# Moving the search for each node's last edge from the token dispatch into the first attention

## The chip, the cores and the metric

The kernel runs on one core of a Trainium2 chip. The metric is the device time of one execution in microseconds, a median over runs. The profile is one further execution with the hardware profiler on. Its engines are PE (TensorE matmul), PEld (TensorE weight load), DVE (VectorE), ACT (ScalarE), POOL (GpSimd) and SP (SyncE, which here only issues transfers).

## The reference, cut to what matters

Four images of 128 channels and 32 by 32 places (1024 places each) go through a chain of attentions, convolutions and expert layers. The parts that matter here:

```python
# first stage, for each of 4 images (n and m run over the 1024 places)
scores = einsum('bcn,bcm->bnm', q, k)
attn   = softmax(scores, axis=-1)
x      = x + einsum('bnm,bcm->bcn', attn, v)
...
# a graph attention further on: 32768 edges with 3 attributes each
eb = edge_attr @ We + be                                # one value of each of 8 heads
col_bias = jnp.zeros((H, N)).at[:, edge_index[1]].set(eb.T)
scores = scores + col_bias[None, :, None, :]
```

Where several edges point at one node, the last one in the list counts. The kernel gets the edges in reversed order, so it looks for the **first** place at which a node's number stands in the list `targets`, and then fetches that edge's three attributes. All of this depends on the inputs alone, on nothing that the stages before compute. A sparse layer between the two stages sends each of the 4096 tokens to two of 16 experts; to do so, a dispatch stage writes the tokens into slots in memory, sorted by expert.

## The kernel before, in words

The program is a chain of stages. Each is a `Stage` (lines 33 to 46): it has its own tiles and semaphores, one block with a program for each engine, and at its end all engines meet. Only then does the next stage begin; POOL clears the semaphores of the stage that ended, one instruction each, ahead of its own work in the next one.

**The first attention** is `one_head_attention` (line 264) with the name `attn0`. It goes over 4 images in a loop, and in each over 8 row tiles `t` of 128 rows. For a tile PE computes the 128 by 1024 scores (L345), DVE takes each row's maximum (L467), ACT the exponentials (L424). PE turns them, eight 128 by 128 pieces into one PSUM tile (L371), DVE copies that to SBUF (L502), PE multiplies with the values (L360), ACT scales by the inverse row sum (L400), which DVE made (`invert`, L489), PE turns the result (L352) and DVE adds it to the activations (`add_turned`, L450). The order on each engine is written out by hand. On DVE, within tile t: wait for the turned tile t, copy it, maximum of t+2, invert t, add t-2. On PE: turn t, scores t+2, multiply t, turn the output of t-1. The output of tile t-1 can be turned only when the addition of t-2 has read the PSUM bank. After the eighth tile DVE adds tiles 6 and 7. SP loads the weights and is idle from then on; POOL copies one image into `xs` at each image's start. All engines run the images as a hardware loop (`Fori`), DVE's at L453. The same function is used a second time, as `attn2`, with a causal mask and other branches.

**The dispatch** is `dispatch_tokens` (line 1577). DVE works out the slots and POOL then sends the tokens, 64 indirect transfers in a row (L1623), and waits until they have landed. ACT's queue loads the experts' weights beside it. A function handed in as `beside` adds to each engine's program what `edge_bias` (line 1462) returns:

- SP loads `raw` (128 by 256 numbers), waits until DVE packed them, stores them as 16-bit numbers, and reads them back in four chunks of 8192, each broadcast to all 128 partitions (2 MB), into two buffers `text`.
- DVE packs them (L1516 to L1525, seven instructions in a chain and two small copies), searches each chunk for eight keys a partition with `max_index` (L1529), combines the four results into one index a node (L1531 to L1539), and later masks, splits and hands over the bias (L1542 on).
- POOL fetches the attributes of the edges found, eight indirect transfers (L1509), and waits for them. They stand in POOL's order in front of the last 16 of the 64 token transfers.

The lines that matter, the wait and the search on DVE, and POOL's order:

```python
        for i in range(CHUNKS):
            dve.wait_ge(chunk_in, 16 * (i + 1))
            dve.max_index(where[:, i, :], text[i % 2][:, CHUNK:CHUNK + KEYS], text[i % 2][:]).then_inc(searched, 1)
...
            for t in range(TILES):
                if t == 3 * TILES // 4:
                    beside_gpsimd(pool)
```

Of the kernel before, what the change touches and what calls it, by code (L numbers as in the profile page):

```python
# [6 lines left out]
F32 = mybir.dt.float32  # L7
# [256 lines left out]
def one_head_attention(m, name, wq, wk, wv, bq, bk, bv, scale, causal, routed=None):  # L264
# [6 lines left out]
    with Stage(nc) as ctx:  # L271
# [16 lines left out]
        zeroed, cleared = m.sem(f"{name}_zeroed", ctx), m.sem(f"{name}_cleared", ctx)  # L288
        block = ctx.enter_context(nc.Block())
# [3 lines left out]
        def _(sp):  # L293
# [20 lines left out]

# [130 lines left out]
        def _(dve):  # L445
# [7 lines left out]
            with dve.Fori(0, B) as b:  # L453
# [36 lines left out]

                maximum(0)
# [3 lines left out]
                for t in range(T):  # L495
# [7 lines left out]
                    if t + 2 < T:  # L503
                        maximum(t + 2)
                    invert(t)
# [956 lines left out]
def edge_bias(m, name, ctx, targets, attributes, we, be, bias_parts):  # L1462
# [3 lines left out]

    nc = m.nc  # L1470
    EDGES = targets.shape[0]
    CHUNK, KEYS = 8192, N // P
    CHUNKS = EDGES // CHUNK
    sb = lambda nm, s, dt=F32: m.sb(f"{name}_{nm}", s, dt, ctx)
    raw, a, c_, short = sb("raw", [P, EDGES // P], I32), sb("a", [P, EDGES // P]), sb("c", [P, EDGES // P]), sb("short", [P, EDGES // P], U16)
    text = [sb(f"text{i}", [P, CHUNK + KEYS], U16) for i in range(2)]
    keys, where = sb("keys", [P, KEYS], I32), sb("where", [P, CHUNKS, KEYS], U32)
    place, miss, best, found, index = sb("place", [P, CHUNKS, KEYS]), sb("miss", [P, CHUNKS, KEYS]), sb("best", [P, KEYS]), sb("found", [P, KEYS]), sb("index", [P, KEYS], U32)
    rows, rowsT, wb = sb("rows", [P, KEYS, 4]), sb("rowsT", [4, N]), sb("wb", [4, HEADS])
    bias, rest, parts = sb("bias", [HEADS, N]), sb("rest", [HEADS, N]), sb("parts", [HEADS, 3, N], BF16)  # L1480
    ps, b_ps = m.psum(f"{name}_ps", [P, N], ctx), m.psum(f"{name}_b", [P, N], ctx)
    dram = nc.dram_tensor(f"{name}_targets", [EDGES], U16, kind="Internal").ap()
    loaded, packed, sent, keyed, keys_set, chunk_in, searched, indexed, ones, masked, turned, kept, summed, split, stored, dve_step = (
        m.sem(f"{name}_{x}", ctx) for x in ("loaded", "packed", "sent", "keyed", "keys_set", "chunk_in", "searched", "indexed",
                                            "ones", "masked", "turned", "kept_", "summed", "split", "stored", "dve"))
    def sync(sp):
        sp.dma_start(raw[:], targets.rearrange("(p e) -> p e", p=P)).then_inc(loaded, 16)
        sp.dma_start(wb[0:3, :], we).then_inc(loaded, 16)
        sp.dma_start(wb[3:4, :], be.rearrange("(o h) -> o h", o=1)).then_inc(loaded, 16)
        sp.wait_ge(packed, 1)  # L1490
        sp.dma_start(dram.rearrange("(p e) -> p e", p=P), short[:]).then_inc(sent, 16)
        sp.wait_ge(sent, 16)
        for i in range(CHUNKS):
            if i >= 2:
                sp.wait_ge(searched, i - 1)
            sp.dma_start(text[i % 2][:, 0:CHUNK], dram[i * CHUNK:(i + 1) * CHUNK].rearrange("(o e) -> o e", o=1).broadcast_to((P, CHUNK))).then_inc(chunk_in, 16)
# [658 lines left out]
```

## Time and profile before

| | us |
|---|---|
| median of 3 runs (2319.66 to 2326.56) | 2325.7 |
| the profiled execution | 2343.5 |
| its span, first to last instruction | 2341.3 |
| PE busy | 1735.8 (74%) |
| DVE busy | 1471.6 (63%) |
| ACT busy | 898.2 (38%) |
| POOL busy | 247.6 (11%) |
| first attention, from its first matmul to the last addition | 25.9 to 207.2 |
| dispatch, from its first load to the next stage's first load | 1219.0 to 1340.3 |

The busy shares are means over stages with quite different limits, so they don't say what a change in one stage is worth. The first attention and the dispatch are far apart in time, and each has to be read by itself: in which order its engines release each other, and which of them is the last to reach the meeting at the stage's end. A line of the timeline gives the start in us, the duration in us, the engine, the line of the program, the operation, its output and inputs, and in brackets how long the engine had been idle and what ended that.

### The profile page before, as it was taken

What the parts mean: (1) busy time and instruction counts of PE and PEld (TensorE: products, weight loads), DVE (VectorE), ACT (ScalarE), POOL (GpSimd) and SP (SyncE); (2) the same over time, 40 slices, a digit from 0 to 9 for tenths busy, and PEclk for the clock granted to TensorE, in tenths of its full rate; (3) what the DMA queues carried; (4) which work ended last, traced back from release to release, by engine and by line L of the source; (5) the groups of instructions that cost most, each with busy time, mean ns of one, the idle gap of its engine ahead of it and who ended that gap; (6) DMA issues with size and microseconds to landing.
All of it is one profiled execution on the core that took longest, in us unless ns stands there. A gap on an engine that the chain in (4) does not pass through costs nothing. (4 is left out here: it accounts for less than half of the span.)

```text
span 2341.3 us, 29974 instructions
## 1 busy us (share of the span) xinstructions
PE 1735.8 (74%) x8782; PEld 819.7 (35%) x8783; DVE 1471.6 (63%) x2899; ACT 898.2 (38%) x1709; POOL 247.6 (11%) x247
## 2 busy tenths in 40 slices
PE   5996986999999573879840199603499999995698
PEld 3774441222222122445530055301122222224576
DVE  4555896878888374366658144325587878865466
ACT  2332332666666330033310033202246666673143
POOL 0001001010001100010006500271100000100000
PEclk9997996999999765979955599856689999997699
DMA  1000244232231401030017132220802332200000
GB/s 42 1 0 11 78 162 72 39 55 47 46 67 26 71 11 45 0 140 0 0 53 246 53 85 67 63 53 30 226 9 49 66 53 51 60 13 0 19 0 36
DMA packets 116162, 125.68 MB, mean 54 GB/s; under 512 B 22675, under 2 KB 93787, under 8 KB 114155
## 3 DMA queue, kind: packets, MB, share of 16 engines
q1 hardware_dynamic: 97822, 101.91, 18.5%
q0 software_dynamic: 13088, 16.46, 2.4%
q10 hardware_dynamic: 5168, 6.29, 0.9%
q8 instruction: 41, 0.67, 0.1%
q14 instruction: 43, 0.35, 0.1%
HBM read 79.92 MB, written 44.22 MB: 53 GB/s over the span
## 5 line engine op out<-in xcount | busy, mean ns | idle before, releaser
L889 DVE TENSOR_REDUCE heads_mx<-heads_n_bank 128x1 f32<-128x1024 f32 (+2 forms) x608 | 631.6, 1081 | 176.6 <-PE heads_n_bank L777 173.4
L871 ACT ACTIVATE heads_prob<-heads_t_bank 128x512 f32<-128x512 f32 (+2 forms) x1120 | 559.1, 578 | 450.0 <-PE heads_t_bank L794 449.9
L777 PE MATMUL heads_n_bank<-heads_ks,heads_qs 96*128 96x512 bf16 (+3 forms) x1120 | 357.9, 400 | 134.0 <-DMA heads_ks<-scale_k_parts 59.5
L794 PE MATMUL heads_t_bank<-heads_qs,heads_ks 99*128 99x512 bf16 (+3 forms) x1120 | 337.0, 381 | 11.9 <-ACT heads_prob L871 8.7
L806 PE MATMUL heads_o_bank<-heads_prob,heads_vs 128*32 128x512 f32 (+2 forms) x2240 | 296.4, 603 | 5.9 <-issue 3.4
L777 PEld LDWEIGHTS heads_n_bank<-heads_ks,heads_qs 96*128 96x128 bf16 (+2 forms) x1120 | 88.3, 100 | 451.7 <-issue 170.2
L794 PEld LDWEIGHTS heads_t_bank<-heads_qs,heads_ks 99*128 99x128 bf16 (+2 forms) x1120 | 106.4, 100 | 206.3 <-ACT heads_prob L871 104.3
L345 PE MATMUL attn_s_bank<-attn_k,attn_q 128*128 128x512 f32 x256 | 123.7, 612 | 0.0
L360 PEld LDWEIGHTS attn_o_bank<-attn_v,attn_probT 128*128 128x128 f32 x800 | 97.7, 192 | 47.1 <-ACT attn_probT L406 25.4
L360 PE MATMUL attn_o_bank<-attn_v,attn_probT 128*128 128x128 f32 x800 | 102.6, 279 | 8.4 <-ACT attn_probT L406 5.0
L260 PE MATMUL ln_ps_bank<-ident,ln_xn 128*128 128x128 f32 x64 | 17.5, 429 | 121.0 <-DVE ln_xn L240 65.6
L1893 DVE SCALAR_TENSOR_TENSOR x_channels<-experts_o_bank,combine,x_channels 128x128 f32 (+1 forms) x256 | 72.5, 345 | 41.7 <-PE experts_o_bank L1849 40.3
L1789 DVE TENSOR_TENSOR experts_hid<-experts_gate,experts_hp_bank 128x256 f32<-128x256 f32 x80 | 33.7, 421 | 99.2 <-ACT experts_gate L1769 99.2
L1728 PE MATMUL experts_hp_bank<-expert_w,experts_xT 128*128 x160 | 90.7, 649 | 5.6 <-ACT experts_xT L1764 2.4
L1078 PE MATMUL in_c_bank<-padded,scale_diag 128*128 128x512 f32 (+1 forms) x198 | 85.1, 590 | 5.1 <-ACT scale_diag L1110 5.1
L205 POOL DMA_INDIRECT ln_got<-routed_y,pick_slots x64 | 61.0, 954 | 193.0 <-issue 193.0
L1849 PEld LDWEIGHTS experts_o_bank<-experts_w,experts_hid 128*128 128x128 f32 x512 | 66.8, 193 | 29.9 <-issue 23.4
L806 PEld LDWEIGHTS heads_o_bank<-heads_prob,heads_vs 128*32 128x32 f32 (+1 forms) x2240 | 45.7, 111 | 82.9 <-issue 73.1
L1868 ACT ACTIVATE experts_hid<-experts_h_bank,experts_b 128x512 f32<-128x512 f32 x64 | 44.0, 688 | 73.1 <-PE experts_h_bank L1855 73.1
L502 DVE COPY attn_probT<-attn_t_bank 128x1024 f32<-128x1024 f32 x32 | 39.2, 1225 | 49.3 <-PE attn_t_bank L371 49.3
L424 ACT ACTIVATE attn_prob<-attn_s_bank,attn_neg 128x1024 f32<-128x1024 f32 x32 | 35.7, 1115 | 89.8 <-DVE attn_neg L467 89.8
L1849 PE MATMUL experts_o_bank<-experts_w,experts_hid 128*128 128x128 f32 x512 | 69.0, 280 | 0.0
(269 smaller groups left out, 2141.7 us busy)
## 6 DMA issues: line engine op xcount, KB each, us to landing
edges_text<-edges_targets SPq DMA_DIRECT2D x4, 2048.0 KB
heads_qs<-scale_q_parts SPq DMA_DIRECT2D x60, 128.0 KB, 4.4
heads_ks<-scale_k_parts SPq DMA_DIRECT2D x60, 128.0 KB, 6.6
routed_x<-attn_zeros SPq DMA_DIRECT2D x3, 2560.0 KB, 13.3
experts_xs<-routed_x SPq DMA_DIRECT2D x24, 320.0 KB, 3.3
heads_wide<-heads_inverse_d POOLq DMA_DIRECT2D x14, 512.0 KB, 8.2
heads_qs<-edge_q_parts SPq DMA_DIRECT2D x48, 128.0 KB
heads_ks<-edge_k_parts SPq DMA_DIRECT2D x48, 128.0 KB
```

The lines of the kernel that those rows point to most:

```text
L205: pool.indirect_dma_start(out=got[:, t, i, :], out_offset=None, in_=routed.y, in_offset=bass.IndirectOffsetOnAxis(ap=slots[:, t:t + 1], ax ...
L345: last = pe.matmul(s_ps[t % 2][:, h * 512:(h + 1) * 512], q[:, t * P:(t + 1) * P], k[:, h * 512:(h + 1) * 512], start=True, stop=True)
L360: last = pe.matmul(o_ps[:, 0:C], probT[t % 2][:, j, :], v[:, j, :], start=(j == 0), stop=(j == n - 1))
L777: last = pe.matmul(ps[0:TN, i * CH:(i + 1) * CH], query(b, slice(0, KB), s, h, j, t * TN, TN), key(b, slice(0, KB), s, j, i * CH, CH), sta ...
L794: pe.matmul(t_ps[i][0:TN, 0:CH], key(of, slice(0, KM), c // NH, j, t * TN, TN), query(of, slice(0, KM), c // NH, c % NH, j, 0, CH), start= ...
L806: last = pe.matmul(o_ps[SLOT * j:SLOT * (j + 1), 0:CH], vs[:, of if whole else 0, t, (4 * s + j) * SLOT:(4 * s + j + 1) * SLOT], prob[i][: ...
L871: act.activation(to[:], t_ps[score_bank(of, place, j)[0]][0:TN, 0:CH], ACT.Exp, scale=scale).then_inc(exped, 1)
L889: dve.tensor_reduce(mx[:, u % UC:u % UC + 1], bank()[0:TN, 0:n], AX.X, ALU.max, negate=True).then_inc(first_used, 1)
L1078: last = pe.matmul(c_ps[:, c * CH:(c + 1) * CH], weights[i].diag[:, tap, :], chunk_window(r, tap, c), start=(tap == 0), stop=(tap == 8))
L1728: pe.matmul(h_ps[j % 2][:], xT[j % 2][:], w12[:, bass.ds(expert, 1), :].rearrange("p o h -> p (o h)"), start=True, stop=True).then_inc(ope ...
L1849: last = pe.matmul(o_ps[e % 2][:, t * P:(t + 1) * P], hid[e % 2][:, t * P:(t + 1) * P], w2s[:, e, :], start=True, stop=True)
L1893: last = dve.scalar_tensor_tensor(out=tile, in0=o_ps[e % 2][:, t * P:(t + 1) * P], scalar=weight, in1=tile, op0=ALU.mult, op1=ALU.add)
```

## The change

The function `edge_bias` is split. What searches goes into a class `EdgeSearch`, whose parts are put into `one_head_attention` for `attn0`; what makes the bias from the fetched attributes stays beside the dispatch.

- The chunks are of 2048 numbers instead of 8192, sixteen instead of four, one after the maximum of every second row tile (four an image). Each of the two text buffers has its own semaphore for loads.
- The packing stands on DVE in front of the first image's first maximum. The combination of the results (now sixteen) stands after the last addition of the fourth image.
- POOL makes the keys in front of the first copy of an image, and fetches the attributes after its last one; it waits for them within the first attention.
- SP's loads, the store and the chunk loads follow the weight loads of the first attention.
- DVE's loop over the images is written out (`range` in place of `Fori`), in both uses of the function.
- Eight semaphores stay with the dispatch; eleven come to the first attention.

```diff
@@ one_head_attention
+        if search:
+            search.place(ctx)
...
             sp.wait_ge(S["loaded"], 16 * (4 if causal else 6))
+            if search:
+                search.sync(sp)
...
         def _(pool):
+            if search:
+                search.prepare(pool)
...
                 pool.tensor_copy(xs[:], at(m.xnT, b + 1)).then_inc(S["staged"], 1)
+            if search:
+                search.gather(pool)
...
-            with dve.Fori(0, B) as b:
+            for b in range(B):
...
+                if search and b == 0:
+                    search.pack(dve)
                 maximum(0)
                 maximum(1)
...
                     if t + 2 < T:
                         maximum(t + 2)
+                    if search and t % 2 == 1:
+                        search.search(dve, b * T // 2 + t // 2)
                     invert(t)
...
                     for t in range(T - 2, T):
                         add_turned(b, t)
+                if search and b == B - 1:
+                    search.choose(dve)
@@ the new class
+class EdgeSearch:
+    CHUNK, KEYS = 2048, N // P
...
+    def sync(self, sp):
+        sp.dma_start(self.raw[:], self.targets.rearrange("(p e) -> p e", p=P)).then_inc(self.loaded, 16)
+        sp.wait_ge(self.packed, 1)
+        sp.dma_start(self.dram.rearrange("(p e) -> p e", p=P), self.short[:]).then_inc(self.sent, 16)
+        sp.wait_ge(self.sent, 16)
+        for i in range(self.chunks):
+            if i >= 2:
+                sp.wait_ge(self.searched, i - 1)
+            part = self.dram[i * self.CHUNK:(i + 1) * self.CHUNK].rearrange("(o e) -> o e", o=1).broadcast_to((P, self.CHUNK))
+            sp.dma_start(self.text[i % 2][:, 0:self.CHUNK], part).then_inc(self.chunk_in[i % 2], 16)
+        for i in range(2):
+            sp.wait_ge(self.chunk_in[i], 16 * self.chunks // 2)
...
+    def gather(self, pool):
+        pool.wait_ge(self.indexed, 1)
+        for r in range(self.KEYS):
+            pool.indirect_dma_start(out=self.rows[:, r, 0:3], out_offset=None, in_=self.attributes,
+                                    in_offset=bass.IndirectOffsetOnAxis(ap=self.index[:, r:r + 1], axis=0)).then_inc(self.m.gathered, 16)
+        pool.wait_ge(self.m.gathered, 16 * self.KEYS)
+        pool.wait_ge(self.ones, 1)
...
+    def search(self, dve, i):
+        if i == 0:
+            dve.wait_ge(self.keys_set, 2)
+        dve.wait_ge(self.chunk_in[i % 2], 16 * (i // 2 + 1))
+        text = self.text[i % 2]
+        dve.max_index(self.where[:, i, :], text[:, self.CHUNK:], text[:]).then_inc(self.searched, 1)
...
@@ edge_bias, dispatch_tokens: what searched is gone
-        for i in range(CHUNKS):
-            dve.wait_ge(chunk_in, 16 * (i + 1))
-            dve.max_index(where[:, i, :], text[i % 2][:, CHUNK:CHUNK + KEYS], text[i % 2][:]).then_inc(searched, 1)
...
-                if t == 3 * TILES // 4:
-                    beside_gpsimd(pool)
```

`pack` and `choose` hold the same instructions as before, on 16 results of a key instead of 4.

## Rows read from the trace of the kernel before

**Rows 1.** Stretches: length, busy time (instructions) of each engine, granted clock, DMA share, GB/s
```profile
25.00:207.00 182.00, 172.43 (x1024) 127.58 (x1024) 92.14 (x132) 60.42 (x107) 3.12 (x3) 1.00 0.00 1
1255.00:1260.00 5.00, 0.00 (x0) 0.00 (x0) 5.00 (x1) 0.00 (x0) 3.86 (x4) 0.50 0.95 361
1290.00:1295.00 5.00, 0.00 (x0) 0.00 (x0) 0.11 (x1) 0.00 (x0) 3.78 (x5) 0.50 0.16 52
```
**Rows 2.** Timeline, the end of the dispatch: POOL's transfers, the next stage's load
```profile
1299.66 1.00 POOL L1509 DMA_INDIRECT edges_rows<-attributes,edges_index  x1 [0.30 <-issue]
...
1308.52 0.95 POOL L1509 DMA_INDIRECT edges_rows<-attributes,edges_index  x1 [0.30 <-issue]
...
1310.95 1.00 POOL L1623 DMA_INDIRECT routed_x<-xn,pick_slots  x1 [1.48 <-DMA edges_rows<-attributes,edges_index]
...
1331.65 0.97 POOL L1623 DMA_INDIRECT routed_x<-xn,pick_slots  x1 [0.30 <-issue]
1340.30 6.75 SPq L1700 DMA_DIRECT2D experts_xs<-routed_x  x8
```
**Rows 3.** Timeline, one row tile of the first attention in the middle of an image
```profile
64.41 1.23 DVE L467 TENSOR_REDUCE attn_neg<-attn_s_bank 128x1 f32<-128x1024 f32 x1 [0.49 <-PE attn_s_bank L345]
65.62 0.27 DVE L450 TENSOR_TENSOR x_channels<-attn_r_bank,x_channels 128x128 f32 x1
67.36 1.23 DVE L502 COPY attn_probT<-attn_t_bank 128x1024 f32<-128x1024 f32 x1 [1.47 <-PE attn_t_bank L371]
68.64 1.99 PEld L360 LDWEIGHTS attn_o_bank<-attn_v,attn_probT 128*128 128x128 f32 x16 [0.43 <-DVE attn_probT L502]
68.88 1.95 PE L360 MATMUL attn_o_bank<-attn_v,attn_probT 128*128 128x128 f32 x16
```
**Rows 4.** Timeline, the last row tile of the first image
```profile
71.85 1.22 DVE L502 COPY attn_probT<-attn_t_bank 128x1024 f32<-128x1024 f32 x1 [3.00 <-PE attn_t_bank L371]
...
75.15 0.27 PE L352 MATMUL attn_r_bank<-ident,attn_out 128*128 128x128 f32 x1
```
**Rows 5.** Timeline, the start of the first image
```profile
25.94 6.65 PE L326 MATMUL attn_s_bank<-attn_xs,attn_w 128*128 128x512 f32 x8 [10.15 <-DMA attn_bvb<-L_conv_bv]
...
34.21 3.60 PE L345 MATMUL attn_s_bank<-attn_k,attn_q 128*128 128x512 f32 x8
34.41 1.22 DVE L459 TENSOR_TENSOR attn_v<-attn_t_bank,attn_bvb 128x1024 f32<-128x1024 f32 x1 [14.46 <-PE attn_t_bank L333]
...
36.12 1.23 DVE L467 TENSOR_REDUCE attn_neg<-attn_s_bank 128x1 f32<-128x1024 f32 x1 [0.49 <-PE attn_s_bank L345]
```
**Rows 6.** Timeline, DVE in the dispatch: packing, wait for text, searches, combination
```profile
1240.61 0.38 DVE L1516 CAST edges_a<-edges_raw 128x256 f32<-128x256 int32 x1
...
1243.45 0.23 DVE L1525 CAST edges_text<-edges_keys 128x8 uint16<-128x8 int32 x2
...
1253.59 0.09 DVE L1529 MATCH_VALUE_LOAD edges_where<-edges_text 128x8 uint16 x1 [9.91 <-DMA edges_text<-edges_targets]
...
1262.33 8.69 DVE L1529 FIND_INDEX8 edges_where<-edges_text 128x8 uint32<-128x8200 uint16 x1
...
1271.00 8.70 DVE L1529 FIND_INDEX8 edges_where<-edges_text 128x8 uint32<-128x8200 uint16 x1
...
1288.40 0.18 DVE L1531 CAST edges_place<-edges_where 128x32 f32<-128x32 uint32 x1
...
1288.83 0.40 DVE L1534 SCALAR_TENSOR_TENSOR edges_place<-edges_place,edges_miss 128x8 f32<-128x8 f32 x4
...
1289.94 0.17 DVE L1539 CAST edges_index<-edges_best 128x8 uint32<-128x8 f32 x1
```
**Rows 7.** Timeline, the end of the first attention and the next stage's first work
```profile
206.93 0.29 DVE L450 TENSOR_TENSOR x_channels<-attn_r_bank,x_channels 128x128 f32 x1 [0.59 <-PE attn_r_bank L352]
207.50 0.33 SPq L2045 DMA_DIRECT2D taps<-L_conv_dw_w  x1
...
209.00 5.44 POOL L2052 MEMSET padded<- 128x4624 f32 x3 [85.92 <-issue]
```
**Rows 8.** Timeline, DVE in the second attention, after a wait for its own result
```profile
1032.70 0.35 DVE L472 SCALAR_TENSOR_TENSOR x_channels<-attn_o_bank,attn_inv,x_channels 128x128 f32 x1 [0.16 <-DVE attn_inv L487]
```

More of the change, by code:

```diff
@@ L1480, in edge_bias @@
+def edge_bias(m, name, ctx, search, we, be, bias_parts):
+    K = EdgeSearch.KEYS
+    sb = lambda nm, s, dt=F32: m.sb(f"{name}_{nm}", s, dt, ctx)
+    rows, rowsT, wb = search.rows, sb("rowsT", [4, N]), sb("wb", [4, HEADS])
     bias, rest, parts = sb("bias", [HEADS, N]), sb("rest", [HEADS, N]), sb("parts", [HEADS, 3, N], BF16)
     ps, b_ps = m.psum(f"{name}_ps", [P, N], ctx), m.psum(f"{name}_b", [P, N], ctx)
[L1482 to L1485, printed above, removed]
+    weighted, masked, turned, kept, summed, split, stored, dve_step = (
+        m.sem(f"{name}_{x}", ctx) for x in ("weighted", "masked", "turned", "kept_", "summed", "split", "stored", "bias_dve"))
@@ L1500, in sync @@
         sp.wait_ge(stored, 16)
-    def prepare(pool):
-        pool.memset(rows[:, :, 3:4], 1.0).then_inc(ones, 1)
-        pool.iota(keys[:], pattern=[[P, KEYS]], base=0, channel_multiplier=1).then_inc(keyed, 1)
-    def gpsimd(pool):
-        pool.wait_ge(indexed, 1)
-        for r in range(KEYS):
-            pool.indirect_dma_start(out=rows[:, r, 0:3], out_offset=None, in_=attributes,
-                                    in_offset=bass.IndirectOffsetOnAxis(ap=index[:, r:r + 1], axis=0)).then_inc(m.gathered, 16)
-        pool.wait_ge(m.gathered, 16 * KEYS)
@@ L1522, in vector @@
-        dve.tensor_copy(short[:], a[:]).then_inc(packed, 1)
-        dve.wait_ge(keyed, 1)
-        for i in range(2):
-            dve.tensor_copy(text[i][:, CHUNK:CHUNK + KEYS], keys[:]).then_inc(keys_set, 1)
-        dve.wait_ge(keys_set, 2)
-        for i in range(CHUNKS):
-            dve.wait_ge(chunk_in, 16 * (i + 1))
-            dve.max_index(where[:, i, :], text[i % 2][:, CHUNK:CHUNK + KEYS], text[i % 2][:]).then_inc(searched, 1)
-        dve.wait_ge(searched, CHUNKS)
-        step(dve.tensor_copy(place[:], where[:]))
@@ L1539, in vector @@
-        dve.tensor_copy(index[:], best[:]).then_inc(indexed, 1)
-        dve.wait_ge(m.gathered, 16 * KEYS)
-        dve.wait_ge(ones, 1)
-        dve.tensor_tensor(rows[:], rows[:], found[:].rearrange("p (k o) -> p k o", o=1).broadcast_to((P, KEYS, 4)), ALU.mult).then_inc(masked, 1)
+        dve.tensor_tensor(rows[:], rows[:], search.found[:].rearrange("p (k o) -> p k o", o=1).broadcast_to((P, K, 4)), ALU.mult).then_inc(masked, 1)
         dve.wait_ge(turned, 1)
@@ L1550, in tensor @@
         pe.wait_ge(masked, 1)
-        for r in range(KEYS):
+        for r in range(K):
             last = pe.transpose(ps[0:4, r * P:(r + 1) * P], rows[:, r, :], m.ident[:])
@@ L2090, in hybrid_kernel @@
             bias_parts = nc.dram_tensor("bias_parts", [3, HEADS, N], BF16, kind="Internal").ap()
-            beside = lambda ctx: edge_bias(m, "edges", ctx, ins["targets"], ins["attributes"], ins["L3_attn_We"], ins["L3_attn_be"], bias_parts)
+            beside = lambda ctx: edge_bias(m, "edges", ctx, search, ins["L3_attn_We"], ins["L3_attn_be"], bias_parts)
             with ExitStack() as inputs:
```

95 lines of the change are left out of this document (56 added, 39 removed).

## Prediction

> **What bounds the kernel now.** The shares of busy time of the whole run don't answer this, since the two places touched lie 1000 us apart. I read the stretches first, then the timeline of each stage's end, then one row tile of the first attention, and asked each time who is last.
>
> In the dispatch the end belongs to POOL. It sends 64 token transfers, one every 1.27 us. The eight attribute fetches stand in its queue before the last sixteen of these: the first starts at 1299.66, and the token transfer behind them at 1310.95, having waited 1.48 us for their landing [rows 2]. The last token transfer is issued by 1331.65 + 0.97 = 1332.6, and the next stage's first load goes out at 1340.30 [rows 2]. DVE's search (1253.6 to 1288.3) and the index after it are ready ten microseconds before POOL comes to the fetches [rows 2, 6]. So of the whole edge work in the dispatch, only the fetches are on the path. The search of some 35 us, its packing and its 9.9 us of waiting for text are covered by POOL's own queue.
>
> In the first attention the end belongs to PE, with DVE close behind. PE is busy 172.4 of 182 us at the full clock (2.4 GHz), DVE 92.1 us [rows 1]. That leaves DVE 90 us idle, which looks like ample room. But a row tile shows how the room is cut up. DVE ends the maximum at 65.64, the inverse and the addition at 65.89, and is then idle 1.47 us until the next turned tile is there; it copies from 67.36 to 68.59, and PE's weight load, which waited for just this copy, starts at 68.64 [rows 3]. The copy is on the path of every tile, and there are 1.47 us of slack before it.
>
> **What is taken away.** Eight fetches and their wait in POOL's queue: 1310.95 - 1299.66 = 11.3 us of the path. The search, the packing and the text loads in the dispatch cost nothing there today, so their removal gives nothing, unless the token transfers get quicker. They come at the same pace, four or five begun in 5 us and 3.8 us busy, while the DMA engines are 95% busy with text and while they are 16% busy [rows 1]. So I give that nothing. Dispatch: **-11.3 us**; the bounds are -10 (the eight at 1.27 without the wait) and -12.
>
> **What is added to the first attention's tiles.** The chunk is of 2048 + 8 instead of 8200 columns. Two searches start 1271.00 - 1262.33 = 8.67 us apart [rows 6]. By columns alone one of 2056 takes 2.17 us; with some 0.1 for the fixed part I take 2.27. Sixteen are 36.3 us of DVE, against 34.7 before.
>
> For tiles 1, 3 and 5 of each image the search stands after the maximum. It starts at 65.64 in the place of rows 3 and ends at 67.91. The inverse and the addition, which used to end 0.25 after the maximum, end at 68.16, and the copy starts at 68.20 instead of 67.36, 0.84 later, and ends at 69.43. PE then multiplies from about 69.6 instead of 68.88 [rows 3], some 0.7 us late. Nothing gives this back, since PE is the next to be full. Queued behind the search are the inverse, on which ACT's scaling waits (not needed before the late multiplication), and the addition of t-2, on which the turn of the output waits (later still). 12 times 0.72 is 8.6 us. Bounds: nothing, if the search fits into idle time, and 27 us if all 2.27 count.
>
> For tile 7 there is no maximum. The copy ends at 71.85 + 1.22 = 73.07, the search at 75.34, the addition of tile 5 at 75.6, and the turn of tile 6's output, at 75.15 before, waits for it [rows 4]. That is about 0.6, four times: 2.4 us. The packing (1240.61 to 1243.68, 3.07 us [rows 6]) begins when DVE has made the values, at 34.41 + 1.22 = 35.63, and ends at 38.70; the first maximum started at 36.12 [rows 5]. The pipeline is empty then, so nothing hides it: 2.6 us.
>
> The loop written out removes register instructions on DVE. In the second attention DVE sits idle 0.16 us before each addition [rows 8]. 32 of them at 0.13 over a plain wait bound the gain at 4 us, and in the other direction the code is straight and I see no cost. Most of those lie before a wait for ACT; I take -0.5. Tiles together: 8.6 + 2.4 + 2.6 - 0.5 = **+13.1 us**.
>
> SP issues the raw load, the store and sixteen chunk loads, in a queue that held nothing after the weights; nothing is queued behind. Each chunk is asked for when the search two before is done, some 9.3 us (two tiles) before it is used. Four times as much text landed within 9.91 us of DVE's last packing instruction, store included [rows 6], so it's there in time; the DMA engines are otherwise idle [rows 1]. POOL's keys and ones come before the first image copy, while the weights are still loading (PE starts at 25.94 [rows 5]): nothing.
>
> **What is added at its end.** This is what I take as decisive. After the last addition (206.93 + 0.29 = 207.2) all engines used to meet within 0.3 us: SP loads at 207.50 [rows 7]. Now three things stand in a row there, and no engine has anything else to do:
>
> - The combination. Before, 1288.40 to 1290.11, 1.7 us [rows 6]. Four additions took 0.40; sixteen take 1.6, and three instructions are 96 columns longer (0.1 each). 1.7 + 1.2 + 0.3 = 3.2.
> - The eight fetches and their landing: 11.3, as above [rows 2].
> - POOL's way out of a stage in which it issued indirect transfers. After the last token transfer 7.7 us pass (1332.6 to 1340.30), of which the landing explains about 1.5, as after the fetches (1309.47 to 1310.95) [rows 2]. The other 6.2 us, against 0.3 in the first attention [rows 7], I put down to POOL closing its transfers, which would come again here: +5.9. Between 0 (it belongs to the dispatch alone, or to the length of its queue) and 6; nothing makes this a gain. I take 5.9, as POOL's queue holds the same kind of transfer.
> - Eleven more semaphores are cleared ahead of POOL's fill of `padded`, which starts 1.8 us after the end, behind 21 clears [rows 7]. At most 0.9; I take 0.5, since SP's twelve loads end at about the same time as the fill.
>
> End: 3.2 + 11.3 + 5.9 + 0.5 = **+20.9 us** (14 to 22).
>
> **Sum.** +13.1 + 20.9 - 11.3 = **+22.7 us** on the profiled execution's span of 2341.3, that is 2364.0. Against the median of the runs, 2325.7 (the profiled one is 0.8% longer), it is 2325.7 + 22.7 = 2348.4 us, slower by 1.0%.
>
> **A rule of the skill against this.** At the start of this stage the granted clock is at the low level (1.2 GHz): eight matmuls take 6.65 us at 25.94 and eight like them 3.60 at 34.21, after PE has worked for some microseconds [rows 5]. The packing makes PE idle 2.6 us longer just after that. If the clock fell back there, a group like the first would be paid again, 3.0 us. The Trainium skill ("TensorE: Matmul & The Clock Gate", "What's actually happening") says that the throttled state is the default and activity releases it, which speaks for such a fall in any new pause. No row of before has a pause of this length inside the stage, so I keep it as a rival.
>
> **The rivals.**
>
> *The search is free* (0.14). 90 us of DVE idle against 36.3 speaks for it; the tight copy speaks against it. 2.6 + 20.9 - 11.3 = +12.2: 2338.
>
> *The search is paid in full* (0.10). If the copy's delay grew through the wait for PE in both directions: 36.3 + 3.1 + 20.9 - 11.3 = +49: 2375. It decides where DVE has no slack before the copy; against it stand the 1.47 us in each tile.
>
> *The clock falls after the packing* (0.08). The likeliest case + 3.0: 2351.
>
> *The way out costs nothing and the search is free* (0.05). 2.6 + 15.0 - 11.3 = +6.3, within 0.3%: 2332.
>
> *Faster: the token transfers get quicker* (0.03). The one thing on the dispatch's path that could be shared with the text's 8 MB is POOL's issue of the 64 transfers. If without the text each took half its 0.97 us of writing, 64 x 0.49 = 31 us go, and the sum is -8.7: 2317. It decides from 22.7 / 64 = 0.36 us a transfer. Against it stands the equal pace beside 95% and 16% of DMA [rows 1].
>
> *The change does not do what it says*, with text late: from 9.3 us a chunk on, DVE would wait in every second tile. A chunk would need as long as four did. That lies within the "paid in full" case and gets no chance of its own.
>
> **How the numbers follow.** The likeliest case (0.60) is 2348. The range, 2334 to 2363, holds it with the bounds of the way out and of the tiles, the free search and the fallen clock; left out are the search paid in full, the quick transfers and the free way out, 0.18 together. About 0.3% (7 us) is what a measurement of this kernel can tell from no change. Faster by more than that: 0.03. Within it: 0.07 (the free way out and a little of the bounds). Slower: 0.90.
>
> **What the profile after would show.** The first maximum of the first image 2.6 us later after the values than before; in tiles 2, 4 and 6 of an image a copy that starts right behind the addition, with no idle time before it; between the last addition and the first load of the next stage some 20 us, with DVE's combination, eight fetches and then nothing for 6 us; in the dispatch 64 token transfers without a break, ending near the same 7.7 us before the next stage. I'm wrong if the copy of every second tile still shows idle time before it (free search), if the load follows the fetches at once (free way out), or if a token transfer takes clearly under 1.27 us.

## Result: slower by 1.6%, and the profile after

| | median | runs | profiled execution, its span |
|---|---|---|---|
| before | 2326.0 us (2319.66 to 2329.44) | 6 | 2343.5, 2341.3 |
| after | 2363.8 us (2354.82 to 2365.94) | 6 | 2359.3, 2357.4 |

The ratio is 1.0159 [1.0138, 1.0180], some 37 us. The forecast was 22.7 us, at 2348.4, with 2363 as the upper end of its range. On the 2325.7 us from which the forecast started the ratio gives 2362.7.

The two profiled spans differ by 16.1 us only. The stage that collects the experts' outputs, which the change does not touch, was 21 us longer in the profiled execution of before. These are its stretches in before and in after (columns: length, busy time of PE, PEld, DVE, ACT and POOL, granted clock, DMA share, GB/s):

```profile
1503.46:1617.24 113.78, 8.74 (x32) 5.72 (x32) 37.36 (x169) 8.44 (x17) 61.04 (x64) 0.50 0.15 37
```
```profile
1536.67:1629.34 92.67, 8.75 (x32) 5.72 (x32) 37.87 (x169) 8.44 (x17) 60.64 (x64) 0.50 0.18 46
```

Engine work is equal, and so are the bytes: 113.78 us at 37 GB/s and 92.67 us at 46 are 4.2 and 4.3 MB. POOL's 64 fetches in this stage took 80.2 us in before and 79.8 in after. What differs is DVE. In before it idled 3 to 10 us in front of several small instructions for which the profile names no engine of this core as the releaser, and fell behind: the stage ended 31 us after the last fetch, in after 10. What held it up stays open. In the later runs the stage took 93 us on one chip with the changed kernel and on another with the kernel before, and 112 to 114 on a third with every kernel. So it belongs to the chip or the execution, and the rest of the two profiles differs by 16.1 + 21.1 = 37.2 us.

I compare stage by stage, from the first instruction after one meeting of the engines to the first after the next:

| | before | after | difference | forecast |
|---|---|---|---|---|
| last addition of the first attention ends | 207.22 | 238.06 | +30.8 | +13.1 |
| from there to SP's first load of the next stage | 0.28 | 15.49 | +15.2 | +20.4 |
| taps stage (the fill of `padded`) | 7.77 | 8.57 | +0.8 | +0.5 |
| dispatch | 121.30 | 108.73 | -12.6 | -11.3 |

So +34.2 us lie where the change was made, and 3.0 elsewhere, of which more below.

**The tiles.** This is a row tile with a search in the second image, all rows of DVE and the TensorE rows that turn tiles (L379) and outputs (L360). Compare [rows 3]:

```profile
109.23 1.23 DVE L475 TENSOR_REDUCE attn_neg<-attn_s_bank 128x1 f32<-128x1024 f32 x1 [0.50 <-PE attn_s_bank L353]
110.37 0.08 DVE L1549 MATCH_VALUE_LOAD edges_where<-edges_text 128x8 uint16 x1
110.44 2.29 DVE L1549 FIND_INDEX8 edges_where<-edges_text 128x8 uint32<-128x2056 uint16 x1
...
112.65 0.14 DVE L497 RECIPROCAL attn_inv<-attn_rows 128x1 f32<-128x1 f32 x1
112.71 0.27 DVE L458 TENSOR_TENSOR x_channels<-attn_r_bank,x_channels 128x128 f32<-128x128 f32 x1
...
113.13 0.30 PE L360 MATMUL attn_r_bank<-ident,attn_out 128*128 128x128 f32 x1 [2.15 <-DVE x_channels L458]
...
113.35 1.06 PE L379 MATMUL attn_t_bank<-ident,attn_prob 128*128 128x128 f32 x8
...
114.45 1.23 DVE L512 COPY attn_probT<-attn_t_bank 128x1024 f32<-128x1024 f32 x1 [1.47 <-PE attn_t_bank L379]
```

DVE was to run from the search straight into the copy. Instead it is idle 1.47 us before the copy, as in before. The idle time is on TensorE, 2.15 us, and what ends it is DVE's addition at 112.71. TensorE turns output t-1 before it turns tile t+1, and for output t-1 it needs `r_ps` free, that is the addition of t-2. That addition stands behind the search. The inverse of tile t stands behind it too, but the scaling that needs it runs from 112.88 to 113.25, beside the turn at 113.13, so it isn't what the turn waited for. In before the turn that follows the addition of [rows 3], which ends at 65.89, is this one:

```profile
66.04 0.30 PE L352 MATMUL attn_r_bank<-ident,attn_out 128*128 128x128 f32 x1
```

In both kernels it starts 0.15 us after the end of the addition (112.98 and 113.13 in after). The table of waits says it for the whole stage (the us in total, how many, the longest); before, after:

```profile
PE attn_r_bank L352 <- DVE x_channels L450: 2.3, 4, 0.6
```
```profile
PE attn_r_bank L360 <- DVE x_channels L458: 21.0, 16, 2.2
```

**The clock.** In before the granted clock was 1.00 through the images [rows 1]. (That row reads 1.00 from 25.00 on although the first record of the clock in this trace is at 31.9; before it eight matmuls took 6.65 us, and eight like them 3.60 later [rows 5].) After shows falls to the lower level (1.2 GHz), of which these four stretches hold one each:

```profile
40.00:44.00 4.00, 4.00 (x12) 2.12 (x13) 1.23 (x1) 1.06 (x2) 0.00 (x0) 0.64 0.82 256
74.00:78.00 4.00, 4.00 (x13) 2.18 (x14) 1.48 (x3) 0.05 (x1) 0.00 (x0) 0.66 0.36 135
173.00:177.00 4.00, 3.15 (x11) 2.41 (x12) 1.82 (x4) 0.37 (x1) 0.00 (x0) 0.66 0.42 131
228.00:232.00 4.00, 4.00 (x21) 4.00 (x21) 0.00 (x0) 0.37 (x1) 0.00 (x0) 0.50 0.00 0
```

**The stage's end** (compare [rows 7] for where it ended, [rows 2] for the fetches), and SP's first load of the taps:

```profile
237.77 0.29 DVE L458 TENSOR_TENSOR x_channels<-attn_r_bank,x_channels 128x128 f32<-128x128 f32 x1 [0.49 <-PE attn_r_bank L360]
237.98 0.22 DVE L1554 CAST edges_spot<-edges_where 128x128 f32<-128x128 uint32 x1
...
240.67 0.17 DVE L1562 CAST edges_index<-edges_best 128x8 uint32<-128x8 f32 x1
241.15 1.19 POOL L1523 DMA_INDIRECT edges_rows<-attributes,edges_index  x1 [102.54 <-DVE edges_index L1562]
...
250.15 0.95 POOL L1523 DMA_INDIRECT edges_rows<-attributes,edges_index  x1 [0.30 <-issue]
253.55 0.33 SPq L2085 DMA_DIRECT2D taps<-L_conv_dw_w  x1
...
256.21 3.95 POOL L2092 MEMSET padded<- 128x4624 f32 x1 [5.11 <-issue]
```

Combination 2.8, fetches 10.3 to the end of the last issue (251.10), then 2.45 us to the load.

**The dispatch.** 64 token transfers from 1283.82, without a break, and the next load 7.0 us after the last (7.7 before):

```profile
1365.97 0.96 POOL L1663 DMA_INDIRECT routed_x<-xn,pick_slots  x1 [0.30 <-issue]
1373.93 2.10 SPq L1740 DMA_DIRECT2D experts_xs<-routed_x  x4
```

### The profile page after: what moved, and what is told of

It reads as the page before. It is cut to its first block and busy times, and to the rows that moved or that the text cites. A ratio compares the mean times of both kernels' runs of the same rounds, so it can differ in the third digit from the quotient of the medians.

```text
span 2357.4 us, 29740 instructions
## 1 busy us (share of the span) xinstructions
PE 1749.9 (74%) x8782; PEld 824.5 (35%) x8783; DVE 1472.9 (62%) x2935; ACT 899.9 (38%) x1709; POOL 246.7 (10%) x247
## 5 line engine op out<-in xcount | busy, mean ns | idle before, releaser
L808 PE MATMUL heads_t_bank<-heads_qs,heads_ks 99*128 99x512 bf16 (+3 forms) x1120 | 339.7, 384 | 11.3 <-ACT heads_prob L885 7.7
L353 PE MATMUL attn_s_bank<-attn_k,attn_q 128*128 128x512 f32 x256 | 123.3, 610 | 0.0
L1762 PE MATMUL experts_xp_bank<-ident,experts_xs 128*128 128x128 f32 x80 | 22.0, 279 | 83.6 <-DMA experts_xs<-routed_x 83.6
L512 DVE COPY attn_probT<-attn_t_bank 128x1024 f32<-128x1024 f32 x32 | 39.1, 1222 | 51.3 <-PE attn_t_bank L379 51.3
## 6 DMA issues: line engine op xcount, KB each, us to landing
routed_x<-attn_zeros SPq DMA_DIRECT2D x3, 2560.0 KB, 13.2
```

What stands on the lines that cost most here:

```text
L353: last = pe.matmul(s_ps[t % 2][:, h * 512:(h + 1) * 512], q[:, t * P:(t + 1) * P], k[:, h * 512:(h + 1) * 512], start=True, stop=True)
L808: pe.matmul(t_ps[i][0:TN, 0:CH], key(of, slice(0, KM), c // NH, j, t * TN, TN), query(of, slice(0, KM), c // NH, c % NH, j, 0, CH), start= ...
```

## Experiments

Each was timed beside the kernel before on one chip, but for the one with half of the transfers, of which there is one execution, its profile. The base is the changed kernel unless said otherwise. The distance from one copy (L512) to the next, tile by tile through the second image, tells most of them apart; in the changed kernel, search_after and short_search every interval with an odd number holds a search, in chunks_1024 every interval:

```
                  0     1     2     3     4     5     6   7 and next image's start
before          4.38  4.48  4.67  4.67  4.67  4.67  4.49  11.65
changed         4.38  5.20  4.33  6.94  4.67  6.94  4.49  12.16
search_after    4.38  5.20  4.33  5.40  4.33  5.40  4.33  11.58
short_search    4.38  4.49  4.67  4.81  4.67  4.82  4.48  11.54
chunks_1024     4.38  4.49  4.68  4.68  4.67  4.67  4.48  11.54
```

### The addition ahead of the search

```
-                    if search and t % 2 == 1:
-                        search.search(dve, b * T // 2 + t // 2)
                     invert(t)
                     elif t >= 2:
                         add_turned(b, t - 2)
+                    if search and t % 2 == 1:
+                        search.search(dve, b * T // 2 + t // 2)
```

> The changed kernel with one thing moved: in the odd tiles DVE searches after the addition of output t-2, not before it. Theory A (the order): TensorE turns output t-1 only after the addition of t-2, and turns tile t+1 only after that; with the addition ahead of the search the search costs what is over the 1.5 us that DVE idles in a tile, some 0.8 us, in every odd tile. Second image (its steadiest) from 49.1 to 45.5 to 47 us, last addition of the stage at 225 to 230 instead of 238.1, falls of the granted clock fewer, whole kernel 2350 to 2356. Rival B (VectorE is simply full): each search costs its 2.3 us wherever it stands in the tile, second image at 49, whole kernel 2361 to 2366.

Measured 2359.3 us beside 2341.0 before, ratio 1.0079 [1.0053, 1.0105]. (The chip's kernel before is 15 us slower than the first chip's, mostly by the collecting stage, so the whole times expected in this run and in those of the cut search, the moved fetches and the loop are low by that; the ratios don't suffer.) The second image took 44.95 us, just under theory A's 45.5, and the last addition ended at 217.1, earlier than A's 225 to 230. The wait of TensorE for the addition is back to before's:

```profile
PE attn_r_bank L360 <- DVE x_channels L458: 2.2, 4, 0.7
```

(The inverse moved ahead of the search together with the addition; by the rows of after above it is the addition that the turn waited for.) DVE now goes from the search into the copy without idle time, which is what the prediction had described for the other order:

```profile
104.28 0.27 DVE L458 TENSOR_TENSOR x_channels<-attn_r_bank,x_channels 128x128 f32<-128x128 f32 x1
104.47 0.08 DVE L1549 MATCH_VALUE_LOAD edges_where<-edges_text 128x8 uint16 x1
104.54 2.29 DVE L1549 FIND_INDEX8 edges_where<-edges_text 128x8 uint32<-128x2056 uint16 x1
106.75 1.21 DVE L512 COPY attn_probT<-attn_t_bank 128x1024 f32<-128x1024 f32 x1
```

The interval is 0.73 us longer, and the next one 0.34 shorter. Order, not DVE's load, made the search dear: 21 us of the stage by two lines changing places (238.1 to 217.1).

### The search cut to 16 columns

```
-        dve.max_index(self.where[:, i, :], text[:, self.CHUNK:], text[:])
+        dve.max_index(self.where[:, i, :], text[:, self.CHUNK:], text[:, self.CHUNK - 8:])
```

> The changed kernel with each search made over the last 8 columns of its chunk and the 8 keys instead of all 2056 columns (its result is not the place of the last edge; that part is left out). Packing, loads of the text, the combination and the fetches stay. Theory A (the searches and what they set off cost all but 2 us of the loop): no fall of the granted clock in the stage, last addition at 208.5 to 210 instead of 238.1, whole kernel 2333 to 2338. Rival B (packing, or the sixteen transfers of the text, or the loop written out carries a share): clock falls stay, last addition at 214 or later, whole kernel above 2341.

A search took 0.17 us. The last addition ended at 211.1, between the two theories and 3.9 us later than in before, and one fall of the clock stayed, the first. Nearly all of the 3.9 us lie at the first image: 2.0 for the packing ahead of its first copy, and 1.7 in the interval behind that copy (6.06 for 4.38 us). So the packing carries a share, as B has it, and the text's transfers and the loop carry none that shows in the other intervals. The whole kernel was 2363.7 beside 2341.0, 1.0100 [1.0074, 1.0127]: 23 us, where the stages touched give 8. That was the first sign of a cost outside them.

### Packing moved ahead of everything

```
+            if search:
+                search.load(sp)
             for i, x in enumerate((wq, wk, wv)):
...
+            if search:
+                search.pack(dve)
             dve.wait_ge(S["loaded"], 16 * (4 if causal else 6))
```

> The changed kernel with the packing of the targets moved ahead of VectorE's waits for weights and values, and the load of the raw targets ahead of the weights: VectorE has nothing else to do there. Theory A (packing costs its own 2 us and then a fall of the granted clock worth 1.7 us): the first image is 3.5 to 4 us shorter (54.5 to 50.5 or 51), the first fall of the clock in the stage (to 0.50 at 52 us) is gone, attention stage 229 to 230 us instead of 233.2, whole kernel 3.5 us less than the changed one. Rival B (the fall comes from the three searches of that image): 2 us less, the fall at 52 us stays. Rival C (the load ahead of the weights holds the whole stage up): the values are made later than 33.8 us and nothing is gained.

(`load` is the first line of `sync`, the raw targets.) The attention stage took 229.4 us, the changed kernel's on the same chip 233.4: 4.0 less, as A said. The first fall is gone. Stretch of the changed kernel run again, then of this one:

```profile
40.00:44.00 4.00, 3.98 (x13) 2.20 (x14) 1.23 (x1) 1.09 (x2) 0.00 (x0) 0.68 0.74 261
```
```profile
40.00:44.00 4.00, 4.00 (x28) 3.23 (x27) 2.14 (x4) 1.46 (x3) 0.00 (x0) 1.00 0.00 0
```

The 13 and the 28 matmuls are not all of one kind. Like for like, the four matmuls of the scores (L353, L355 in the second kernel) took 3.15 us at 40.95 in the first and 1.88 at 38.87 in the second. Before the fall PE had been idle for 2.91 us, in the kernel that packs early for 0.84. The fall stood in all six profiles that pack after the values, whatever their searches cost, and in neither of the two that pack early. The whole kernel was 1.0171 [1.0139, 1.0203] beside 1.0197 for the changed one: the right sign, though the intervals overlap.

### The fetches moved to a later stage

```
-            if search:
-                search.gather(pool)
...
                 pool.memset(v[:, p, :].rearrange("p (t d) -> p t d", d=SLOT)[:, :, HD:SLOT], 1.0).then_inc(ones, 1)
+            search.gather(pool)
```

> The changed kernel with the eight row fetches of POOL moved on to the stage that makes the head inputs of the scales (125 us, POOL has two memsets in it). Theory A: the fetches stood alone at the end of the attention stage, so its end comes 0.4 to 1 us after the combination: 241.2 to 241.8 instead of 253.4, that is 12 us less, whole kernel 2350 to 2354, the later stage within 0.5 us of its 125.2. Rival B: the fetches cost in their new stage what they cost in the old (POOL's way out after them, or the stores of that stage held up): the sum stays at 2361 to 2366.

The attention stage took 220.3 us instead of 233.3, 13.0 less. SP loads 0.3 us after the combination, and the new stage is no longer than before (124.3 us):

```profile
240.16 0.17 DVE L1562 CAST edges_index<-edges_best 128x8 uint32<-128x8 f32 x1
240.62 0.33 SPq L2085 DMA_DIRECT2D taps<-L_conv_dw_w  x1
```

Theory A for the stage. The whole kernel, 1.0130 [1.0098, 1.0162] or +30 us, is again more than the stages explain (+20).

### The loop written out, alone

```
-            with dve.Fori(0, B) as b:
+            for b in range(B):
```

> The kernel before with VectorE's loop over the images written out, nothing else. Theory A: 0.3 us a turn less in both attention stages, some 0.7 to 1.5 us less in all, 2324 to 2325.5. Rival B: instructions that are met for the first time are slower to arrive, and part of the first attention stage's growth is that: 2 to 8 us more than before.

0.9995 [0.9978, 1.0013]. The first attention stage is 185.3 instead of 187.1 us, the second as before (159.5). A in sum, not in place. The interval reaches from 5 us less to 3 us more, so it is the two edited stages themselves that speak against B.

### Half of the token transfers

```
-                for slots in picks.slots:
+                for slots in picks.slots[:1]:
```

> The changed kernel with one of the two transfers of each token tile in the dispatch (32 instead of 64, the tokens of the second pick are not sent, that part is left out). It measures POOL's way out of the stage: from the end of the last transfer's issue to SP's next load it took 7.0 us after 64 transfers. Theory A (about 0.083 us for each indirect transfer of the stage): 4.2 to 4.5 us after 32. Theory B (a fixed wait of some 6 us, as the prediction had it): 6.8 to 7.2 us. The dispatch stage is some 40 us shorter in either.

```profile
1334.38 0.95 POOL L1663 DMA_INDIRECT routed_x<-xn,pick_slots  x1 [0.30 <-issue]
1339.73 3.31 SPq L1740 DMA_DIRECT2D experts_xs<-routed_x  x5
```

4.40 us from the last issue to the load: theory A. The trace has a drain instruction on POOL at the end of each stage, which the views do not list. It took 0.71 us after 8 indirect transfers (the attention stage of after), 2.68 after 32 (here), 5.29 after 64 (the dispatch of after) and 5.94 after 72 (the dispatch of before), that is some 0.083 us for each.

### The changed kernel once more

> The changed kernel as it is, once more, so that the edits to it stand beside it on one chip and what its profile repeats can be told from what it doesn't. Theory A (the stages that the change touches repeat, the rest is chance): first attention stage 233 us long within 1, taps stage 8.6, dispatch 108.7 within 0.5; the stage that collects the experts' outputs, 113.8 before and 92.7 after, comes out by the chip and not by the kernel; ratio to the kernel before 1.014 to 1.018. Rival B (the change shortened that stage by 21 us): it is 92 to 94 us long again.

2370.0 us beside 2323.9, 1.0197 [1.0166, 1.0229] or 46 us. First attention 233.4, taps 8.6, dispatch 108.9, falls of the clock worth the same 7.8 us, in part in other tiles; the collecting stage 93.1 (before: 93.2 on another chip of the same pace). The stages touched give +35 at most. The many-headed attention, two stages, took 448.6 and 454.4 us, and 443.8 and 447.3 in before. Theory A for the touched stages. The 93.1 us of the collecting stage alone would fit rival B; the kernel before with 93.2 and the changed kernels with 112 to 114 on the third chip rule it out. "The rest is chance" is doubtful.

### Reserving what the change reserves

The change keeps `edges_rows` and `edges_found`, 160 bytes a partition, for the whole program, and 64 KB of memory from its start. Three kernels put these into the kernel before:

```
+        m.sb("ahead_rows", [P, N // P, 4], F32)
+        m.sb("ahead_found", [P, N // P], F32)
```
```
+        m.targets_dram = nc.dram_tensor("edges_targets", [ins["targets"].shape[0]], U16, kind="Internal").ap()
```

The first is before_tiles; before_tiles_512 makes the second tile 96 numbers wide; the other line, at the program's start, is before_dram.

> The kernel before itself, a second time beside its own runs, for a profile on the same chip. It says how much of a difference is chance: ratio 0.998 to 1.002, its two stages of many-headed attention 444 and 447 us long within 3.

> The kernel before with the two tiles that the change puts in for the whole program (128 x 32 and 128 x 8 numbers) reserved and not used, so that all later tiles lie where the changed kernel has them. The changed kernel, beside the kernel before on one chip, took 46 us more, and the stages that it touches account for 35; the two stages of many-headed attention that it doesn't touch were 445 and 447 us before, and 447 and 451 in the mean of its variants. Theory A (this is chance at the boundaries of those stages): ratio 0.998 to 1.002. Theory B (the shifted tiles lengthen them): 1.003 to 1.005, some 7 to 11 us more.

> The kernel before with the 64 KB of packed targets reserved in memory ahead of everything else, as the changed kernel has them, and not behind the queries and keys of the many-headed attention. Theory A (chance at the boundaries of the untouched stages): ratio 0.998 to 1.002. Theory C (the shifted addresses in memory lengthen the loads of those stages): 1.003 to 1.005, some 7 to 11 us more, with the two stages at 447 to 454 us.

> The kernel before with 512 bytes a partition reserved for the whole program instead of the 160 of the run before this, which took 1.0031 of the time of the kernel before. Theory A (160 bytes put all later tiles on addresses that are no multiple of 64 bytes, and that costs): with 512 bytes they are multiples again, ratio 0.998 to 1.0015. Theory B (any reserved tile costs, or that the tiles lie elsewhere at all): 1.002 to 1.005, as with 160 bytes. Both two stages of many-headed attention are looked at: 444 to 446 in A, one of them 448 or more in B.

| | ratio to before | wait for the sums, us |
|---|---|---|
| before_again | 0.9999 [0.9980, 1.0019] | 27.0 |
| before_dram | 1.0002 [0.9990, 1.0014] | 26.8 |
| before_tiles (160 bytes) | 1.0031 [1.0017, 1.0045] | 34.4 |
| before_tiles_512 | 0.9999 [0.9983, 1.0014] | 27.5 |

Two tiles that nobody reads cost 7.2 us (3.9 to 10.4 by the interval). The last column is a wait that grew by as much: DVE's for the row sums of the many-headed attention, which POOL sends to memory and back. 12 such waits are counted in the two stages. 160 bytes, then 512:

```profile
DVE heads_inverse L936 <- DMA heads_spread<-heads_sums_d: 34.4, 12, 3.7
```
```profile
DVE heads_inverse L936 <- DMA heads_spread<-heads_sums_d: 27.5, 12, 3.7
```

The wait, and the length of the two stages from one meeting to the next, over all fourteen profiles:

| bytes reserved | profiles | wait for the sums, us | both stages together, us |
|---|---|---|---|
| none | 4 | 26.8 to 32.8 | 887.6 to 891.9 |
| 512 | 1 | 27.5 | 887.7 |
| 1216 (the last kernel below) | 1 | 31.7 | 889.6 |
| 192 (the moved fetches) | 1 | 36.1 | 896.8 |
| 160 | 7 | 34.0 to 40.7 | 893.0 to 904.0 |

So 160 bytes go with longer stages in every profile, but not by a steady amount: from before to after the wait is 32.1 and 34.0 us and the stages 890.7 and 893.0; 40.7 and 902.9 us are the changed kernel run again. 512 bytes shift every later tile too and cost nothing beside the kernel before on their chip, so it is not the shift as such, against theory B.

Which addresses are good ones is not shown. The Trainium skill ("DMA: Bandwidth & Descriptors", "How a descriptor splits into AXI transactions") says that a piece of a transfer that doesn't start at a multiple of 256 bytes costs extra beats; the runs agree in so far as 512 is such a multiple and 160 isn't. But 192 and 1216 bytes leave the same remainder at 256, and both are multiples of 64, and they came out on different sides. The addresses of the tiles themselves are not in the traces. So theory A holds only in its number: 512 bytes cost nothing, and its reason stays open.

### Every step where its engine idles

The packing early, 32 chunks of 1024, each search after the addition, in every tile; the combination in the taps stage, where DVE had no work; the fetches in the stage of the head inputs.

```
-    CHUNK, KEYS = 2048, N // P
+    CHUNK, KEYS = 1024, N // P
...
                         add_turned(b, t - 2)
+                    if search:
+                        search.search(dve, b * T + t)
...
+                @block.vector
+                def _(dve):
+                    search.choose(dve)
```

> The changed kernel with every step of the search put where its engine idles: the packing ahead of VectorE's first wait, 32 chunks of 1024 targets, one after the addition in every row tile (1.2 us each in the 1.5 us that VectorE idles there), the combination in the taps stage where VectorE has no work, the row fetches in the stage of the head inputs. Theory A (only what outlasts the idle time costs): tiles as long as in the kernel before, attention stage 185 to 188 us, taps stage 7.8, dispatch 108.5, whole kernel 11 to 15 us under the kernel before, ratio 0.9935 to 0.9955. Rival B (the text's arrival, 32 waits and issues, and the search's fixed part eat the margin): tiles 0.3 to 0.6 us longer, attention stage 196 to 205, ratio 0.999 to 1.003. Rival C (work beside the attention makes the granted clock fall though no tile is longer): falls of the clock in the stage and 5 us or more of it.

2314.0 us beside 2323.9, 0.9963 [0.9943, 0.9983]: 9 us faster than before, 56 faster than the changed kernel on that chip. The attention stage took 185.8 us, the taps stage 8.6, the dispatch 108.5; the clock did not fall. A search fits into the idle time, with 0.26 us left of the 1.47:

```profile
94.32 0.27 DVE L462 TENSOR_TENSOR x_channels<-attn_r_bank,x_channels 128x128 f32<-128x128 f32 x1
94.51 0.08 DVE L1551 MATCH_VALUE_LOAD edges_where<-edges_text 128x8 uint16 x1
94.57 1.23 DVE L1551 FIND_INDEX8 edges_where<-edges_text 128x8 uint32<-128x1032 uint16 x1
96.06 1.23 DVE L514 COPY attn_probT<-attn_t_bank 128x1024 f32<-128x1024 f32 x1 [0.26 <-PE attn_t_bank L381]
```

The stages give -13.3 against the profile of before; the ratio gives -8.7 (-13.2 to -4.0), short of A's 11 to 15. The taps stage took 0.8 us more than A's 7.8. The other 4.6 us are not placed. The kernel reserves 1216 bytes for the whole program, but its wait for the sums, 31.7 us, is the shortest on that chip (38 to 41 in the others, all with 160), so nothing shows that it pays for them.

## Why the prediction was off

**What bounds the kernel: right for the dispatch, half right for the tile.** That only the fetches are on the dispatch's path held: -12.6 against -11.3. Half of the 1.3 between them is POOL's drain, 0.66 shorter with eight transfers fewer. The other half is the series of the 64 itself: the median step from one token transfer to the next went from 1.272 to 1.265 us, and without the fetches the series is 0.7 us shorter. That is far from the 0.36 us a transfer of the rival.

**The tiles, +13.1 forecast, +30.8 measured.** This is the step that failed. The prediction asked of the inverse and the addition, queued behind the search, who waits for them, and answered for the addition of t-2: the turn of the output, "later still". It isn't later. The code issues the turn of output t-1 right before the turn of tile t+1, on an engine that works in order. In before the addition ended at 65.89 and the turn behind it started at 66.04, too close to be a wait that a table shows (2.3 us, 4 times), and without slack. The 1.47 us before the copy [rows 3] were slack of DVE only behind the addition; ahead of it there was none. Term by term:

- Tiles 3 and 5 of each image: 8 times 2.27 = 18.2, where 8 of the 12 x 0.72 stood, 5.8. The run with the addition ahead shows 0.73, the very number: the sum was made for that order.
- Tile 1 has no addition, and its 0.72 came out exactly (5.20 against 4.48), in part by luck: by the prediction's own lines the copy is 0.84 late, and "about 69.6" for the multiplication rounds that down to 0.72. But the next interval is 0.34 shorter. "Nothing gives this back" was wrong by half, 1.4 us in all.
- Tile 7: 0.5 for 0.6. Packing: 2.0 for 2.6, by the rows 1.71 us from values to maximum before [rows 5] and 3.72 after.
- Falls of the clock: 7.8 us, for which the sum held nothing. 1.7 belong to the packing, the rival with a chance of 0.08 and a price of 3.0. It came true, at little more than half the price. The rule of the Trainium skill that it leaned on ("TensorE: Matmul & The Clock Gate", "What's actually happening": the throttled state is the default, activity releases it) agrees with the fall to 0.64 in the stretch behind the packing, which packing early took away. The other 6.1 us, of falls in later tiles, came in every kernel that searches 2056 columns ahead of the addition; with the addition first the second and third image had none and the fourth kept one, of 1.6. So most of them are a second price of the same waits on TensorE.

18.2 + 1.5 + 2.0 + 2.0 + 7.8, less 0.7 for values made earlier, is 30.8.

**The stage's end, +20.9 forecast, +16.0 measured.** Combination 2.8 for 3.2, clears 0.8 for 0.5, both fine. POOL's way out was the error on the other side: 5.9 taken from 64 + 8 transfers, 0.7 found after 8. The lower bound named the cause ("it belongs to the dispatch alone, or to the length of its queue") and I took the upper one; the run with half of the transfers shows the price of each. Landing and leaving together took 2.45.

**Outside: some microseconds, forecast nothing.** Two tiles of the program's length stood in the diff and were passed over as memory, not time. Alone they cost 7.2 us. The profiles of before and after leave only 3.0 for everything outside, the changed kernel run again 11, the one with the cut search 15. So the 7.2 is the best single price, and not a sum that closes.

With it, 30.8 + 16.0 - 12.6 + 7.2 = 41.4, between the 37 and the 46 us that the two measurements of the change gave. The errors were +17.7 in the tiles, -4.9 at the end, -1.3 in the dispatch and +7.2 outside; the range's upper end had room for the bounds of one term, and not for all searches in full. That the first measurement still lies at the edge of the range (2362.7 beside 2363) is in part luck: the price of the way out, too high by 5.2 us, offset part of the tiles, too low by 17.7.

**The rivals.** "The search is free" and "paid in full" were both drawn as properties of DVE's idle time. What decided was a place in a queue: in full in tiles 3 and 5, a sixth of its length in tile 1, nothing for chunks of 1024. The check that the prediction itself named, a copy without idle time before it in every second tile, was the right one: it failed at 114.45 with its 1.47 us.

## What to carry to other kernels

Idle time before an instruction is room only for work that is queued behind everything another engine waits for: before work is put ahead of a small instruction, look for the next thing in the *waiting* engine's own order, and let the small one go first. Cut the filler to the gap (1.2 us into 1.5, not 2.3 into 1.5), and put what can't be cut, packing, combination and fetches, where its engine has no work and none waits for it. A tile that is kept for the whole program moves all others: it can cost time far from where it is used, as 160 bytes did here and 512 did not, so time the reservation by itself.

## What the hardware did that I had not expected

- POOL's drain at the end of a stage grows by 0.083 us for each indirect transfer issued in it (0.71, 2.68, 5.29 and 5.94 us for 8, 32, 64 and 72). After the 64 fetches of the collecting stage it ends 5.29 us after the last of them too, in before and in after. Other stages have drains of up to 7.0 us without any such transfer, so this is not all that a drain can hold.
- 160 unused bytes ahead of most tiles cost 7.2 us (1.0031), 512 none (0.9999).
- On DVE two instructions over 8 columns took 2.62 and 1.11 us, in the combination moved to the taps stage, where the like took 0.17:

```profile
208.69 5.49 POOL L2104 MEMSET padded<- 128x4624 f32 x3 [86.69 <-remote]
...
210.04 2.62 DVE L1567 TENSOR_SCALAR edges_found<-edges_best 128x8 f32<-128x8 f32 x1
...
212.70 1.11 DVE L1568 TENSOR_SCALAR edges_best<-edges_best 128x8 f32<-128x8 f32 x1
```

  They end at 212.66 and 213.81, within 0.05 us of POOL's first and second memset (208.69 + 3.95 = 212.64, and 213.77). The Trainium skill ("SBUF — State Buffer", "SBUF: two separate sides") describes a pair of ports that POOL and certain DVE instructions share, held by whoever comes first for its whole instruction; these rows agree with it. Not every DVE instruction waits: the two-input ones (L1564) beside the start of the first memset kept their 0.18 us. It cost nothing that shows, since the fill ends at the same time and the stage took 8.6 us, as in after.
